# A language-model tower on one core: windowed attention rebuilt around scores computed twice, with the softmax maximum and exponential taken over four PSUM banks at once

## The reference, cut to what matters

```
Q, K, V = x@wq, x@wk, x@wv                   # 16 heads of 16 dims
local: query i sees keys i-63 .. i           # window 64
   p = softmax(mask(Q K^T / 4)); local = p V
GQ = x@wgq; GK, GV = mean over 8 tokens of x@wgk, x@wgv    # 8 heads, 64 latents
remote: latent n is seen by token s if n <= s // 8
   rem = softmax(mask(GQ GK^T / 4)) GV; rem = rem @ r_out_w
out = (sigmoid(Q.gl) * local + sigmoid(Q.gr) * rem) @ w_out
```

## Time and profile before

| what | value |
|---|---|
| time, median of 3 executions | 5002.72 us (4962.28 to 5036.0) |
| span of the profiled execution, first to last instruction | 4945.8 us |
| instructions | 80440 |
| busy: PE, PEld, DVE, ACT, POOL | 94%, 62%, 49%, 33%, 15% |
| mean granted clock of TensorE | 0.773 of 2.4 GHz |

### The profile page before, as it was taken

How to read it: one execution, slowest core, us unless ns; L and a number is a source line. 1 busy time by engine, 2 the same in 40 slices (tenths; PEclk the granted TensorE clock), 3 DMA queues, 4 the chain that set the end, 5 groups by cost and what they waited for, 6 DMA issues and landing times. The chain is left out here.

```text
span 4945.8 us, 80440 instructions
## 1 busy us (share of the span) xinstructions
PE 4629.6 (94%) x27948; PEld 3051.0 (62%) x27948; DVE 2406.4 (49%) x7255; ACT 1623.1 (33%) x3333; POOL 739.8 (15%) x817
## 2 busy tenths in 40 slices
PE   5999999999999999999999999999996699999999
PEld 3666666666666666666666666666664366665666
DVE  4444444444444444534444444444445766666661
ACT  2333333333333333323333333333332233333333
POOL 1000000000000000100000000000000244444443
PEclk8777676776767676868676776767676799999999
DMA  1000000000000000000000000000000011111111
GB/s 36 14 10 10 10 11 10 10 9 10 11 10 9 10 11 10 15 9 11 10 11 10 10 10 10 10 10 10 10 11 27 20 51 52 47 50 51 48 42 41
DMA packets 52864, 94.25 MB, mean 19 GB/s; under 512 B 9116, under 2 KB 37736, under 8 KB 52488
## 3 DMA queue, kind: packets, MB, share of 16 engines
q0 software_dynamic: 18816, 51.41, 3.7%
q1 hardware_dynamic: 33672, 37.87, 2.3%
HBM read 55.68 MB, written 33.55 MB: 18 GB/s over the span
## 5 line engine op out<-in xcount | busy, mean ns | idle before, releaser
L1320 DVE TENSOR_REDUCE mx<-S_ps 128x4 f32<-128x512 f32 (+1 forms) x640 | 442.7, 692 | 1343.1 <-PE S_ps L914 1102.9
L914 PE MATMUL S_ps<-Kt,Qt 32*64 32x128 f32 (+1 forms) x6144 | 1090.7, 374 | 0.0
L687 ACT ACTIVATE probT<-T_ps 128x512 f32<-128x512 f32 x640 | 382.2, 597 | 1919.9 <-PE T_ps L963 1916.6
L914 PEld LDWEIGHTS S_ps<-Kt,Qt 32*64 32x64 f32 (+1 forms) x6144 | 634.0, 186 | 532.9 <-issue 463.9
L963 PE MATMUL T_ps<-cst,prob 128*128 128x128 f32 x2560 | 564.6, 360 | 0.0
L963 PEld LDWEIGHTS T_ps<-cst,prob 128*128 128x128 f32 x2560 | 381.9, 181 | 230.2 <-issue 230.2
L847 PE MATMUL S_ps<-hT,w 128*128 128x512 f32 x1024 | 474.7, 610 | 17.1 <-ACT hT L654 12.1
L860 PE MATMUL O_ps<-w,hid 128*128 128x256 f32 x2048 | 460.3, 379 | 0.0
L1321 DVE TENSOR_TENSOR prob<-S_ps,mx 128x512 f32<-128x512 f32 x640 | 442.6, 692 | 21.8
L936 PEld LDWEIGHTS O_ps<-Ve,probT 128*64 128x64 f32 x4096 | 359.8, 172 | 124.9 <-issue 124.9
L691 ACT ACTIVATE prob<-prob 128x512 f32<-128x512 f32 x640 | 401.0, 627 | 102.6 <-DVE prob L1321 102.2
(11 more groups left out here) (205 smaller groups left out, 5913.3 us busy)
## 6 DMA issues: line engine op xcount, KB each, us to landing
h_rows<-h SPq DMA_DIRECT2D x128, 128.0 KB, 1.7
w<-in_w SPq DMA_DIRECT2D x16, 1024.0 KB, 6.1
rows<-in_tok_table,idx_now POOLq DMA_INDIRECT x136, 3.6
out_rows<-orow,idx_cur POOLq DMA_INDIRECT x128, 2.4
b<-in_b SPq DMA_DIRECT2D x8, 128.0 KB, 5.1
hrow<-h_rows,idx_next POOLq DMA_INDIRECT x64, 2.8
hrow<-h_rows,idx_cur POOLq DMA_INDIRECT x64, 2.7
P<-in_pos_table SPq DMA_DIRECT2D x1, 512.0 KB
```

The lines of the kernel that those rows point to most:

```text
L687: nc.scalar.activation(probT[u % 2][:, :], T_ps[u % 2][:, :], ACT.Copy).then_inc(s_pT, 1)
L914: mm = nc.tensor.matmul(cols[lo:hi, n:n + 2, a, :], Qt[par][r:r + 32, c, t * P + lo:t * P + hi], Kt[par][r:r + 32, c, block, :, :], start= ...
L1320: chain(dve, nc.vector.tensor_reduce(top, sc, AX.X, ALU.max), base)
```

## The change

Five units per sequence take the place of twenty. Unit 0 holds the latent attention of all four tiles, units 1 to 4 hold all 16 heads of one token tile. A unit fills four banks (`banks`, 128 x 2048), the memory of S_ps and T_ps together; bank g belongs to the strip of 32 contraction rows g.

- `top_scores` computes mask and scores with queries on the partitions: 16 bf16 matmuls of 32 rows x 64 columns that stream 512, and 32 float32 matmuls of 32 x 64 that stream 128 (unit 0: 64 of them that stream 64). The eight places of such a tile are gone through in turn.
- `dve_tops` reduces all 2048 columns to maxima with one instruction. Task MX transposes the maxima (4 or 2 transposes), ScalarE copies them with scale -1 into `low`, and SP sends them by two DMAs into spare rows of Qt or Gq, against a row of ones in Kt or Gk. Thus the second scores come out with the maximum subtracted.
- `key_scores` computes the scores again with keys on the partitions, into the same four banks: 16 mask matmuls, then 16 float32 matmuls that stream 128 and 32 that stream 64 (unit 0: 8 that stream 512).
- `act_exp` takes one exponential of 128 x 2048 from PSUM to `probT` or `latT`. The transposes of probabilities, their copies and the subtraction are gone.
- `values` does a tile's 32 matmuls of local heads and 8 of latents in one go.
- The plan has ten halves (`half(n)` issues the tasks of half n; VAL is a tile's `values`). TensorE's order for s in 0..4: top scores of unit s, half 2s, key scores of unit s-1, half 2s+1. MX stands last in every even half. Normalizations of embedded rows and of `h1` (xn, y) move from VectorE to POOL. The query projections Q and G and the key projections K and PK are emptied by two ScalarE instructions each. Masks are sent packed in the constant table.
- The loop body is four sequences, run 7 times; sequences 0, 1, 30 and 31 and the draining body are written out.

```diff
-        S_ps = [ctx.enter_context(nc.psum_tensor(f"S_ps{j}", [P, 512], F32)) for j in range(2)]
-        T_ps = [ctx.enter_context(nc.psum_tensor(f"T_ps{j}", [P, 512], F32)) for j in range(2)]
+        banks = ctx.enter_context(nc.psum_tensor("banks", [P, 4, 512], F32))
+        S_ps, T_ps = [banks[:, j, :] for j in (0, 1)], [banks[:, j, :] for j in (2, 3)]
...
+        plan = [
+            [("MT", 1), ("ET", 0), ("ET", 1), ("VAL", 2), ("ET", 2), ("ET", 3), ("YT", 0), ("WO", 1), ("MX", 0)],
+            [("RT", 2), ("Q", 0), ("SC", 0), ("RO", 2)],
+            [("MT", 2), ("VAL", 3), ("YT", 1), ("WO", 2), ("MX", 1)],
+            [("RT", 3), ("Q", 1), ("SC", 1), ("RO", 3)],
+            [("MT", 3), ("G", 0), ("PK", 0), ("YT", 2), ("WO", 3), ("MX", 2)],
+            [("K", 0), ("V", 0), ("SC", 2)],
+            [("VAL", 0), ("YT", 3), ("MX", 3)],
+            [("RT", 0), ("K", 1), ("PV", 0), ("SC", 3), ("RO", 0)],
+            [("MT", 0), ("VAL", 1), ("WO", 0), ("MX", 4)],
+            [("RT", 1), ("V", 1), ("V", 2), ("V", 3), ("RO", 1)],
+        ]
...
+                        if name == "MX" and m.here(task):
+                            sp.wait_ge(s_mA, m.out(task))
+                            for j in range(2):
+                                if s == 0:
+                                    sp.dma_start(Gq[q % 2][HD * (1 - j)::32, j, :].rearrange("p (t k) -> p t k", t=TS),
+                                                 lowl[j::2, :, :]).then_inc(s_low[s], 16)
+                                else:
+                                    sp.dma_start(Qt[q % 2][HD * (1 - j)::32, j, :, (s - 1) * P:s * P],
+                                                 low[(s - 1) % 2][j::2, :, :]).then_inc(s_low[s], 16)
...
+        def pool_norm(pool, n, t, hb, m):
+            pool.wait_ge(s_var0, TS * n + t + 1)
+            nc.gpsimd.tensor_tensor(out=rs0[:, t:t + 1], in0=ve0[:, t:t + 1], in1=mhalf[:, :],
+                                    op=ALU.pow).then_inc(s_rs0, 1)
+            pool.wait_ge(s_rs0, TS * n + t + 1)
+            if m is not None:
+                pool.wait_ge(s_misc, m.done(("ET", t)))
+            stand(pool)
+            nc.gpsimd.tensor_scalar(xn[:, t, :], hres[:, hb, t, :], mv0[:, t, 0:1], rs0[:, t:t + 1],
+                                    ALU.subtract, ALU.mult).then_inc(s_xn, 1)
...
+            elif name == "MX":
+                if t == 0:
+                    nc.scalar.activation(lowl[:, :, :], bank[0:2 * G, :].rearrange("p (t k) -> p t k", t=TS),
+                                         ACT.Copy, scale=-1.0).then_inc(s_mA, 1)
+                else:
+                    nc.scalar.activation(low[(t - 1) % 2][:, :, :], bank[0:2 * G, 0:KC * P].rearrange("p (c k) -> p c k", c=KC),
+                                         ACT.Copy, scale=-1.0).then_inc(s_mA, 1)
...
+        def act_exp(act, k, u):
+            act.wait_ge(s_ST, k + 1)
+            dst = latT if u == 0 else probT[(u - 1) % 2]
+            nc.scalar.activation(dst[:, :, :], banks[:, :, :], ACT.Exp).then_inc(s_exp, 1)
...
+            elif name == "MX":
+                pe.wait_ge(s_max, NU * b + t + 1)
+                if t == 0:
+                    tops = mxl[:, :].rearrange("p (g j t) -> p t (g j)", g=G, t=TS)
+                else:
+                    tops = mx[:, t % 2, :].rearrange("p (g j c) -> p c (g j)", g=G, c=KC)
+                for n in range(TS if t == 0 else KC):
+                    mm = nc.tensor.transpose(bank[0:2 * G, n * P:(n + 1) * P], tops[:, n, :], c_ident)
...
+            strip = [slice(32 * g, 32 * (g + 1)) for g in range(G)]
+            side = [slice(0, W), slice(W, P)]
...
+            def top_scores(m, b, par, s):
...
+                    pe.wait_ge(s_mA, m.out_before(("K", 1)))
+                if not (isinstance(b, int) and NU * b + s < 2):
+                    pe.wait_ge(s_exp, NU * b + s - 1)
+                t = s - 1
+                for r in range(2):
+                    for g in range(G):
+                        for a in range(2):
+                            if s == 0:
+                                nc.tensor.matmul(banks[side[a], g, :].rearrange("p (j t n) -> p j t n", j=2, t=TS),
+                                                 onehot[strip[g], r, :],
+                                                 lat_query[strip[g], a, r, :, :].unsqueeze(1).to_broadcast([32, 2, TS, NL]),
+                                                 start=r == 0, stop=False)
+                            else:
+                                nc.tensor.matmul(banks[side[a], g, :].rearrange("p (h k) -> p h k", h=G),
+                                                 onehot[strip[g], r, :],
+                                                 by_query[strip[g], min(t, 1) if a == 0 else 1, r, :].unsqueeze(1)
+                                                 .to_broadcast([32, G, P]), start=r == 0, stop=False)
+                for n in range(2 * TS if s == 0 else G):
+                    j, c = divmod(n, TS if s == 0 else KC)
+                    for g in range(G):
+                        for a in range(2):
+                            if s == 0:
+                                at_ = c * P + a * W
+                                mm = nc.tensor.matmul(banks[side[a], g, n * NL:(n + 1) * NL],
+                                                      Gq[par][strip[g], j, at_:at_ + W], Gk[par][strip[g], j, :],
+                                                      start=False, stop=n == 2 * TS - 1)
+                            else:
+                                at_ = t * P + a * W
+                                mm = nc.tensor.matmul(banks[side[a], g, n * P:(n + 1) * P],
+                                                      Qt[par][strip[g], j, c, at_:at_ + W],
+                                                      Kt[par][strip[g], j, c, at_:at_ + P],
+                                                      start=False, stop=n == G - 1)
...
+            def key_scores(b, par, u, drained):
+                pe.wait_ge(s_max, drained)
+                pe.wait_ge(s_low[u], 32 * b + 32)
+                t = u - 1
+                for r in range(2):
...
+                    return
+                at_ = t * P
                 for n in range(G):
+                    j, c = divmod(n, KC)
+                    for g in range(G):
+                        k, q = Kt[par][strip[g], j, c, :], Qt[par][strip[g], j, c, :]
+                        nc.tensor.matmul(banks[side[0], g, n * P:(n + 1) * P], k[:, W + at_:P + at_], q[:, at_:at_ + P],
+                                         start=False, stop=n == G - 1)
+                        nc.tensor.matmul(banks[side[1], g, n * P:n * P + W], k[:, at_:W + at_], q[:, at_:at_ + W],
+                                         start=False, stop=False)
+                    for g in range(G):
+                        k, q = Kt[par][strip[g], j, c, :], Qt[par][strip[g], j, c, :]
+                        mm = nc.tensor.matmul(banks[side[1], g, n * P + W:(n + 1) * P], k[:, P + at_:P + W + at_],
+                                              q[:, at_ + W:at_ + P], start=False, stop=n == G - 1)
+                mm.then_inc(s_ST, 1)
...
+            def values(b, par, t):
+                pe.wait_ge(s_O, TS * b + t + 1)
+                pe.wait_ge(s_exp, NU * b + t + 2)
+                for n in range(G):
+                    j, c = divmod(n, KC)
+                    for g in range(G):
+                        h = 8 * c + 2 * g + j
+                        for a, vals in ((0, Ve[par]), (1, Vo[par])):
+                            nc.tensor.matmul(O_ps[t % 2][side[a], h * OW:(h + 1) * OW],
+                                             probT[t % 2][:, g, n * P + a * W:n * P + (a + 1) * W],
+                                             vals[:, t, h, :], start=True, stop=True)
+                for g in range(G):
+                    at_ = (H + 2 * g) * OW
+                    for a in range(2):
+                        mm = nc.tensor.matmul(O_ps[t % 2][side[a], at_:at_ + 2 * OW],
+                                              latT[:, g, t * P + a * W:t * P + (a + 1) * W],
+                                              bdV[par][:, g, :, :].rearrange("p a d -> p (a d)"), start=True, stop=True)
                 mm.then_inc(s_PV, 1)
...
+                    if m.new:
+                        top_scores(m, b, par, s)
+                    half(2 * s)
+                    if m.old if s == 0 else m.new:
+                        drained = NU * b + s + 1 if m.new else NU * SEQS
+                        if s == 0:
+                            key_scores(b - 1, 1 - par, NU - 1, drained)
+                        else:
...
+        def dve_tops(dve, k, s):
+            dve.wait_ge(s_S, k + 1)
+            tops = mxl[:, :] if s == 0 else mx[:, s % 2, :]
+            nc.vector.tensor_reduce(tops.rearrange("p (g h) -> p g h", g=G),
```

(67 more changed lines are left out.)

507 lines of the change are left out of this document (215 added, 292 removed).

## The result

The changed kernel takes 3429.2 us (median of 4 runs, 3422.3 to 3433.1); before, run beside it, takes 5009.3 (4962.3 to 5036.0). The ratio is 0.685, 95% interval 0.681 to 0.690. That is 500 us under the forecast of 3930 and 71 us under the low end of its range. A second set of executions gave 3433.1 us beside 4989.7, ratio 0.690 (0.685 to 0.695). The profiled execution of after took 3433.06 us, 2.2 more than its span.

A forecast was written before the change was run, and what follows sets the result against it. TensorE was taken to bound the kernel. 32 sequences of 81 us, 26 for loop returns, 1249.5 outside the attention and 5 for tables gave a span of 3873 us; plus 57, 3930 us. Range 3500 to 4650.

The forecast's parts named there:

- Direction and mechanism of the scores: Score matmuls on TensorE: all eight tiles, four strips by two column halves, run side by side; 16.5 us a sequence.
- 68 us a sequence at full clock: Attention, per sequence: 53.7 us of TensorE work plus 14.5 us of exposed waits, all at full clock.
- the exposed waits: TensorE idle per sequence: bank handovers around the maximum 2.7, odd halves behind the exponential 7.8, semaphores 4; 14.5 us.
- I take 0.6, near what is seen: Share of the attention's work at full clock: 0.6 x 68 + 0.4 x 101 = 81 us a sequence.
- the prediction's own factor of 1.8: TensorE work at half clock takes 1.8 times its full-clock time; mask and scores showed 1.75.
- The 57 us: Added to the 3873 us span, because before's median of 5002.7 lies 57 above its profiled span of 4945.8.
- Unchanged 1249.5 + 5 us: Time outside the attention stays at 1249.5 us, plus 5 us for longer constant tables.
- all at full clock: Case with the whole attention at full clock, 32 x 68: 3514 us in total.
- Instructions are the limit: Rival: top and key scores take 0.03 us a record, 28.3 us a sequence in place of 16.5; 4155 us; chance 0.14.
- Open ring: Rival: maximum and exponential stand uncovered in each unit on the four shared banks; 96 us a sequence, 4410 us; chance 0.2.
- Strips in turn: Rival: row strips run one after another, scores 56 us in place of 16.5; 127 a sequence, 5400 us; chance 0.12.
- the full-clock sum of before: Before's TensorE work per sequence at full clock: 58 us of units plus 25.4 of other tasks, 83 us.

The follow-up runs named there:

- the first experiment: The changed kernel with its score matmuls reordered so that one strip of 32 rows is finished before the next begins; same instructions and banks: 5434.4 us.
- the quarter stream: The kernel before with one 512-column bf16 matmul over a single strip of 32 rows added to each mask: 5580.8 us, ratio 1.126.
- the runs with two: The changed kernel with each maximum done twice, 3613.6 us, and in a separate run with each exponential done twice, 3931.6 us.
- experiment 5434: The changed kernel with the strip outermost in top and key scores, one strip of 32 rows after another: 5434.4 us, same run as the first experiment.
- the two orders tried: The changed kernel with RO and SC ahead of Q and task RT ending the even half, 3471.5 us; then with RT ahead of WO, 3420.4 us.

## Why the prediction was wrong, step by step

- *Direction and mechanism of the scores:* right. Side by side was the forecast, and the eight tiles do run so. The Trainium skill, TensorEngine Tiling (Array Packing), Key Properties, says so for tiles in general; the starts 0.02 us apart agree for strips too, which no row of before could show, and the first experiment shows that it holds only if neighbours in the order lie in different tiles.
- *Sizes on TensorE:* top scores 1.6 forecast, 1.55 measured; key scores 1.7 and 1.86; values 2.5 and 1.88 + 0.57 = 2.45. The maximum 2.3 and 2.29; the exponential 1.9 and 1.88.
- *68 us a sequence at full clock:* close; 276.2 / 4 less a quarter of the loop's 3.1 us stop is 68.3. Some 30 us of that pass are at half clock, so at full clock throughout it would be nearer 65: the exposed waits, 14.5 us forecast, were overcounted by about 3 (an estimate). That the 68 for full clock throughout lies so near the measured 69 at a clock of 0.94 is in part luck: too much waiting stood in for the missing clock.
- *"I take 0.6, near what is seen":* the step that failed. The share of work at full clock was carried over from a kernel whose TensorE work was of another kind. The granted clock of after's attention is 0.94, which by the prediction's own factor of 1.8 means that some 0.93 of the work ran at full clock (an estimate). The sum had 32 x 81 + 26 = 2618 us for the attention, the trace has 2205.9: 412 of the 500 us. I did notice that half clock appears with TensorE busy all the while the earlier trace rows, and did not ask which work was in the array then. The units of before put their scores into one strip at a time; after puts them into all four. That the kind of work in the array moves the clock is shown: mask twice in before, with nothing else changed, lifts it (0.69 to 0.88, 8.5% faster), and the order of the strips alone takes after from 0.94 to 0.63. That it is the filling of the array fits these two, the run without masks (0.65, slower) and the quarter stream (0.65, 12.6% slower). It does not explain after without masks (0.97) or the third mask (0.88 still), so as a rule it is argued and not shown.
- *Other readings of the clock.* How busy TensorE is does not order the runs: 96 to 97% busy goes with 0.63, 0.65, 0.69 and 0.88, and 87% with 0.94. Nor does the number of matmul records in 1000 us: 5693 go with 0.65, 6988 with 0.88, 10468 with 0.63. After also has fewer transposes, since those of the probabilities are gone; that alone does not lift the clock, as strips in turn has none of them either. Whether it does part of it was not tried.
- *The 57 us* between before's span and its median: wrong too. Executions of after take some 2 us more than their spans; if before's do, the profiled one took 4948 us, less than all four that were timed (4962.3 to 5036.0). Single executions of before range from 4901 us at a clock of 0.782 to 5035 us at 0.758: what I added as a constant goes with the clock, which varies from run to run; after's runs lie between 3422 and 3438 over eight. After's median lies 2 us under the profiled span, so this term is 59 us too high.
- *Unchanged 1249.5 + 5 us:* 1225.0, so 30 less. The stage behind the attention took 34 less (1178.0 to 1143.6), the one ahead of it 10 more; this was not looked into.
- These three add up: 412 + 59 + 30 = 501. The case "all at full clock", 3514, was much the nearer one; with the 59 and the 30 off it gives 3425, and the attention's 4 us over 32 x 68 + 26 make it 3429.
- *Rivals.* Instructions are the limit: not as priced. 64 records of L1013 take 1.08 us, 0.017 each, where the rival had 0.03. The Trainium skill, TensorE: Matmul & The Clock Gate, in "Wait — 56ns, not 53.3ns?", has 25 ns as the least distance; the trace does not agree where tiles lie side by side, with 0.017 us a record. Open ring: no; the row of the pass leaves 34.8 us in which TensorE is idle, 8.7 a sequence, where the rival had 21 for maximum and exponential alone. More of either is paid, as the runs with two show. Strips in turn: no, and as an experiment 5434 us where the rival said 5400; that nearness is in part luck, since the clock was 0.63 and not as in the rival's sum.
- *How much of the gain is what.* By the full-clock sum of before, 83 us a sequence, and after's 68.9, the attention's 1490 us divide into (115.5 - 83) x 32 = 1040 us of clock and (83 - 68.9) x 32 = 450 us of work, waits included. By that the clock is the larger part. The 83 is my sum, so the split is an estimate; the experiments show the clock's part in kind and direction, not its whole size.

Open: why the masks of after can go without the clock falling (0.97); why a third mask in before does not lift it; what exactly decides the level; and what bounds the 8.7 us a sequence in which TensorE is idle, where removing waits in the two orders tried returned next to nothing. The version with RT ahead of WO is the fastest found with the mask in place, by 0.4%, which I would not call a gain.

## What to carry to other kernels

Before forecasting a kernel whose TensorE stream changes in kind, look at the granted clock of each stretch together with how many rows and columns of the array its matmuls use, and forecast with both levels; a share of full clock does not carry over from one mix to another. In these runs small tiles ran side by side only if neighbours in program order lay in different tiles, and here the price of losing that was paid twice, in time and in clock (pace 132.4 for 69.1, clock 0.63 for 0.94). Check whether the profiled execution is a typical one of its kernel before adding the difference to a sum.

## What was not expected of the hardware

- An added 128x128 matmul of 512 bf16 columns in each unit made the kernel faster by 8.5% (clock 0.71 to 0.87 over the loop, TensorE busy at 96% or more in both).
- Eight 32x64 float32 tiles together start a record each 0.017 us: 64 in 1.08 us, beside 0.06 for each pair of 128x64 records in the values.
- Lengthening ScalarE's piece by 9.4 us a sequence cost 15.6, with the clock at 0.86 in place of 0.95; and behind the 3.1 us stop at the loop's return the clock was 0.58 over 20 us (1.2 GHz for most of it), with TensorE busy for 16 of them.
